# A one-core decoder layer: context values as 32-column weights, no transposes of the attention result, and four work lists rewritten

## What is computed

```python
x = x + gated_linear_attention(layernorm(x), ...)   # conv, silu, 8 heads, causal, decay
x = x + xattn(layernorm(x), ctx, ctx, Wq, Wk, Wv, Wo)
x = x + ffn(layernorm(x), w_router, w_block)        # the best 48 of 64 positions only

# xattn, 16 heads of 8 features:
q = heads(Q @ Wq.T); k = heads(K @ Wk.T); v = heads(V @ Wv.T)
attn = softmax(q k^T / sqrt(8))
return merge(attn @ v) @ Wo.T
```

## Time and profile before

| | |
|---|---|
| median of 3 runs | 335.04 us |
| profiled execution | 332.23 us |
| its span, first to last instruction | 330.5 us |
| PE busy / DVE / ACT / POOL | 274.6 / 240.0 / 245.9 / 163.7 us |
| mean granted PE clock | 0.985 |

### The profile page before, as it was taken

One profiled execution on the slowest core, in us unless ns is written; L12 is line 12 of the kernel. 1 busy time (PEld: TensorE's weight loads), 2 busy tenths in 40 slices (PEclk: granted clock), 3 DMA queues, 4 the chain that ended last, 5 costly groups with the idle time before them and its releaser, 6 DMA issues.

```text
span 330.5 us, 10717 instructions
## 1 busy us (share of the span) xinstructions
PE 274.6 (83%) x4184; PEld 195.9 (59%) x4184; DVE 240.0 (73%) x588; ACT 245.9 (74%) x438; POOL 163.7 (50%) x226
## 2 busy tenths in 40 slices
PE   1697868879998899888999899889987997898861
PEld 1576636655677566655776478556854684465540
DVE  1577788689578968896789677976697657656554
ACT  6399868976988698769976997699769875862611
POOL 5145366834755445574657375728551625023630
PEclk9998999999999999999999999999999999999996
DMA  3830200020003000300020001300110010001010
GB/s 73 234 99 18 67 0 6 13 69 2 4 13 86 2 3 12 96 10 1 11 73 4 0 10 33 93 1 9 33 45 2 5 43 16 2 0 34 2 32 17
DMA packets 15730, 10.52 MB, mean 32 GB/s; under 512 B 2816, under 2 KB 13952, under 8 KB 15680
## 3 DMA queue, kind: packets, MB, share of 16 engines
q1 hardware_dynamic: 15680, 9.84, 11.2%
HBM read 4.79 MB, written 2.10 MB: 21 GB/s over the span
## 4 chain that ended last, share of the span: by engine, by line
PE 34%; issue 13%; DVE 13%; ACT 12%; POOL 7%; POOLq 0%; ACTq 0%; DVEq 0%
PE S L824 6%; PE PT L861 6%; PE PB L882 6%; ACT pr L1259 3%; PE PA L766 3%; ACT prT L1266 3%; ACT L1183 2%; PE S L839 2%; DVE nmax L1627 2%; DVE at L1573 2%; PE PT L646 2%; PE PA L782 2%; POOL rs L399 2%; POOL yout L523 2%; DVE st L1476 1%
## 5 line engine op out<-in xcount | busy, mean ns | idle before, releaser
L1627 DVE TENSOR_REDUCE nmax<-S 128x16 bf16<-128x1024 f32 x31 | 37.9, 1221 | 29.0 <-PE S L824 29.0
L1266 ACT COPY prT<-PT 128x512 f32<-128x512 f32 x62 | 36.1, 582 | 15.8 <-PE PT L861 14.8
L861 PEld LDWEIGHTS PT<-ident,pr 128*128 128x128 f32 x248 | 26.4, 140 | 29.0 <-issue 17.8
L861 PE MATMUL PT<-ident,pr 128*128 128x128 f32 x248 | 39.9, 283 | 4.2 <-ACT prT L1266 2.3
L1147 ACT ACTIVATE k_bd<-S,k_rows 128x512 f32<-128x512 f32 (+1 forms) x72 | 41.9, 645 | 0.4 <-PE S L671 0.2
L824 PE MATMUL S<-k_bd,qT 64*64 64x512 f32 x248 | 33.7, 613 | 5.5 <-ACT pr L1259 2.6
L882 PE MATMUL PB<-v_x,prT 128*64 128x18 f32 x992 | 37.3, 213 | 0.5 <-ACT prT L1266 0.2
L882 PEld LDWEIGHTS PB<-v_x,prT 128*64 128x64 f32 x992 | 32.8, 137 | 8.1 <-issue 6.8
L1259 ACT ACTIVATE pr<-S,rs 128x1024 f32<-128x1024 f32 x31 | 34.5, 1114 | 3.4 <-PE S L839 2.7
L486 POOL TENSOR_TENSOR kc<-ke,e_r 128x512 f32<-128x512 f32 x32 | 34.9, 1109 | 3.7 <-issue 3.7
L766 PEld LDWEIGHTS PA<-v_bd,at 128*64 128x64 f32 x512 | 16.6, 137 | 19.4 <-DVE at L1573 13.9
(11 more groups left out here) (171 smaller groups left out, 669.1 us busy)
## 6 DMA issues: line engine op xcount, KB each, us to landing
cT<-in_ctxT SPq DMA_DIRECT2D x7, 256.0 KB, 3.6
v_bd<-vt SPq DMA_DIRECT2D x28, 64.0 KB, 2.1
out<-yout SPq DMA_DIRECT2D x7, 256.0 KB, 3.8
q_bd<-qs SPq DMA_DIRECT2D x96, 8.0 KB
cT<-in_ctxT SPq DMA_DIRECT2D x2, 128.0 KB, 2.6
x_all<-in_x SPq DMA_DIRECT2D x1, 256.0 KB, 2.9
v_bd<-vt SPq DMA_DIRECT2D x8, 32.0 KB, 2.1
out<-yout SPq DMA_DIRECT2D x2, 128.0 KB, 3.3
```

The costliest lines, as they stand in the source:

```text
L861: last = nc.tensor.transpose(dst[:, P * p:P * p + P], pr_v[:, i % 2, P * (hp * n + p):P * (hp * n + p) + P], ident[:, :])
L1266: nc.scalar.copy(prT[:, 512 * n:512 * n + 512], pt_buf(g, n)[:, :]).then_inc(s_prT, 1)
L1627: nc.vector.tensor_reduce(nmax[:, XH * (i % 2):XH * (i % 2) + XH], cut(s_buf(g, i), XH, L), AX.X, ALU.max, negate=True).then_inc(s_max, 1)
```

## The change

The operands of `x_values` change places: `v_x` is the weight, 32 columns per head pair, and a piece of `prT`, 64 columns, is the stream. Four head pairs of a half fill the four 32-row bands of `PB`, so the result has features as rows. The 16 values of a pair stand in columns 16 to 31 of its 32, with zeros ahead of them; half n = 0 reads a window 16 columns further on, so that the two halves fall on different rows of a band and are accumulated. A second weight, `den_of` (ones and zeros), with all 128 columns of `prT` as the stream, writes each feature's denominator beside it. Per half there are 12 matmuls where there were 8.

```diff
-                for p in range(hp * n, hp * n + hp):
-                    for half in range(2):
-                        last = nc.tensor.matmul(dst[L * half:L * half + L, 2 * VC * p:2 * VC * p + 2 * VC],
-                                                prT_v[:, p, L * half:L * half + L], v_xv[:, g % 2, 2 * i + half, p, :],
-                                                start=True, stop=True)
+                ahead = VB // 2 * (1 - n)
+                for half in range(2):
+                    for q in range(hp):
+                        p = hp * n + q
+                        nc.tensor.matmul(dst[VB * q:VB * q + VB, L * half:L * half + L],
+                                         v_xs[:, g % 2, 2 * i + half, VB * p + ahead:VB * p + ahead + VB],
+                                         prT_v[:, p, L * half:L * half + L],
+                                         start=n == 0 and half == 0, stop=n == 1, skip_group_check=True)
+                for q in range(hp):
+                    last = nc.tensor.matmul(dst[VB * q:VB * q + VB, P:2 * P], den_of[:, ahead:ahead + VB],
+                                            prT_v[:, hp * n + q, :], start=False, stop=n == 1, skip_group_check=True)
                 last.then_inc(s_PV, 1)
 
-            def x_out(g):
-                pe.wait_ge(s_cx, start(g + 1))
-                pe.wait_ge(s_prT, 2 * start(g + 1))
-                to_features(g, PT, cx).then_inc(s_CX, 1)
-
             def x_out2(g):
-                pe.wait_ge(s_cxT, g + 1)
+                pe.wait_ge(s_cx, start(g + 1))
...
-            def b_out(g):
-                act.wait_ge(s_CX, g + 1)
-                nc.scalar.copy(cxT[:, 0:cols(g)], PT[:, 0:cols(g)]).then_inc(s_cxT, 1)
...
-                nc.vector.reciprocal(mine, pv[:, :, XD:VC]).then_inc(s_rden, 1)
+                mine = rden[:, P * (i % 2):P * (i % 2) + P]
+                nc.vector.reciprocal(mine, pv[:, P:2 * P]).then_inc(s_rden, 1)
                 dve.wait_ge(s_rden, start(g) + i + 1)
                 if i == 0:
-                    dve.wait_ge(s_CX, g)
-                nc.vector.tensor_tensor(cx[:, E * i:E * i + E].rearrange("p (h v) -> p h v", h=XH), pv[:, :, 0:XD],
+                    dve.wait_ge(s_WO, g)
+                nc.vector.tensor_tensor(cxT[:, P * i:P * i + P], pv[:, 0:P], mine, ALU.mult).then_inc(s_cx, 1)
```

More of the change, by code:

```diff
@@ L984, in first @@
                 attend(1, 1, 1)
+                project_g(2)
+                x_scores(0, 1)
+                x_attend(0, 0, 0)
+                less_max(0, 1)
+                x_attend(0, 0, 1)
+                project_v(2)
+                x_values(0, 0, 0)
+                context_values(2)
+                aug_weights(2)
+                x_values(0, 0, 1)
                 x_attend(0, 1, 0)
-                project_v(2)
-                x_values(0, 0, 1)
+                context_keys(2)
                 x_attend(0, 1, 1)
+                transpose_o(1)
                 x_values(0, 1, 0)
                 x_values(0, 1, 1)
-                context_values(2)
-                aug_weights(2)
-                context_keys(2)
-                x_out(0)
-                project_g(2)
-                transpose_o(1)
-                x_out2(0)
                 gla_out(1)
                 transpose_x(3)
+                x_out2(0)
                 queries(1)
@@ L1034, in step @@
                 x_scores(n, 3)
+                x_values(n, 1, 1)
                 x_attend(n, 2, 0)
-                x_values(n, 1, 1)
-                x_attend(n, 2, 1)
-                less_max(n, 3)
                 if has(a + 1):
                     transpose_x(a + 1)
+                less_max(n, 3)
+                x_attend(n, 2, 1)
+                gla_out(b)
                 x_values(n, 2, 0)
@@ L1094, in last @@
                 keep_awake(8, 20)
-                x_out(7)
+                queries(8)
                 x_out2(7)
-                queries(8)
-                keep_awake(8, 21)
                 queries2(8)
@@ L1124, in last @@
                 ffn(8)
+            def last():
+                pass
             run(first, opening, step, closing, last)
@@ L1310, in opening @@
                 a_keys(0, 0)
+                a_values(0)
+                a_keys(0, 1)
                 a_qk(0)
@@ L1367, in opening @@
                 a_v(2)
-                a_square(1)
                 b_probs(0, 1, 1)
-                a_spread(1)
-                a_deviation(1)
-                a_values(2)
-                b_out(0)
                 a_keys(2, 0)
-                a_gates(2)
+                a_keys(2, 1)
                 a_features(3)
+            def opening():
+                pass
             def step(n):
                 a, b, c = n + 2, n + 1, n - 1
-                a_keys(b, 1)
                 a_gate(b)
@@ L1383, in step @@
                 a_keys(b, 2)
+                a_keys(b, 3)
                 b_queries2(n)
+                a_values(b)
                 a_aug(b)
-                a_keys(b, 3)
                 a_silu(a)
@@ L1461, in last @@
                 b_probs(8, 1, 1)
-                b_out(8)
                 b_ffn(8)
@@ L1914, in closing @@
                 b_own(7)
-            def last():
                 b_ranks(7)
```

484 lines of the change are left out of this document (236 added, 248 removed).

## The result

The changed kernel takes 342.4 us (median of 4 runs, 341.1 to 344.6) where the kernel before took 334.3 beside it: a ratio of 1.027, 95% interval 1.022 to 1.032. It is slower. The forecast was 331 us where the profiled execution before had 332.2, so no change that can be told; 342.4 lies near the upper end of the whole range, which the slower rivals held, but outside the forecast's own, 326 to 338, and the time moved the other way.

What follows compares the result with a forecast made beforehand. No engine is full; a chain through several engines around the never-free score buffer sets the step. Opening -1.5, loop +0.1 and end +0.3 gave -1.1 us on 332.2: 331 us, range 322 to 343.

Steps and rivals of the forecast that it cites:

- the opening part: Everything ahead of step 1: DVE's wait for x_rest given back, then 3.9 us instead of 5.44 after scores(2, 0); -1.5 us.
- five terms: Changes to the score buffer's five uses per step: +0.3, -0.4, +0.4, +0.8 and -1.0 us, summing to 0.1 over six steps.
- tile 1: Second use of the score buffer: maximum waits behind head norm, yet 6.3 us against 6.74, -0.4; sign, DVE wait near 2 us.
- tile 0: First use of the score buffer: PE's work between successive scores takes 5.6 us against 5.34, +0.3.
- tile 2: Third use of the score buffer: next scores wait for x_values(n, 1, 0), which needs tile 0 weighed; 5.05 us against 4.64, +0.4.
- The end: From weighing the last tile to the last x_out2: longer weighing and a selection stand ahead on DVE, +0.3 us.
- The reciprocal: On DVE, growing from 16 to 128 elements per row: 0.95 us each, 2.8 us more DVE work per step.
- The swapped matmuls: A half of x_values on PE with four bands side by side: 0.5 us, +0.04; 0.65 to 0.7 in a single run.
- The cheap reciprocal: Rival: the longer reciprocal on DVE costs only 0.37 us, giving 324 us; chance 0.16.
- Two bands at a time: Rival: only two PE bands run side by side, 0.9 us a half, +0.45, giving 342 us; chance 0.10.
- DVE as the bound: Rival: half of DVE's new 2.8 us a step does not fit its waits, +1.4 a step, 339 us; chance 0.16.
- Better lists: Rival: the new order hides more, without the tiles' waits, -1.1 us a step, 324 to 325 us; chance 0.12.

Runs made afterwards that it cites:

- e14: The changed kernel itself, unedited, measured again beside the other runs: 342.3 us, ratio 1.025 to the kernel before.
- e6: Changed kernel with a_stats(2) on DVE and scale_a(2) on POOL moved later, as in the kernel before, so nothing ahead waits for x_rest: 340.2 us, 1.020.
- e9: Changed kernel with POOL's kc products of group 1 waiting for group 2's silu, and scores(1, 0) later on PE: 340.7 us, 1.023.
- e4: Changed kernel with a reciprocal of 128 x 16 elements in place of 128 x 128, the other divisors being ones: 333.4 us, 0.998.
- e12: Changed kernel with POOL's first kc of a step also waiting for DVE's gl of that step: 342.9 us, 1.031.
- e8: Kernel before, with old operands and short reciprocals, in the new instruction lists: 341.8 us, 1.024.
- e1: Kernel before with the swapped matmuls, long reciprocal and wider clear in its old lists, x_out and b_out taken out: 333.6 us, 1.001.
- e11: Kernel before with a reciprocal of 128 x 128 elements in place of 128 x 16, the added results read by nobody: 343.6 us, 1.033.
- e10: Changed kernel with the edits of e6 and e9 together: 338.2 us, 1.017.
- e2: Changed kernel with the opening part's lists of the kernel before and the new lists from step 1 on: 350.1 us, 1.048.

## Why the prediction was wrong, step by step

**The step that failed** is the opening part: "gives the 2.5 us back, so these transfers start at the same time by my walk", priced at -1.5 us, measured +5.75 (4.6 between the means under e14). The transfers start 7.37 us late. The walk had seen DVE's wait for `x_rest` rightly (4.42 us at 14.8 to 19.2), but it is not given back: without it the transfers start 2.6 us earlier and step 1 1.4 to 2.5 us earlier (e6). The walk had left out the head norm and the maximum that now stand between `a_log(2)` and `a_scaled_q(2)`, 2.0 us by the rows of both kernels. And it had carried over each duration from the trace of before without asking what POOL does at that moment in the new order; e9 shows 2.9 us of that at the silu, but not at the transfers, where e9 holds up the masks instead. How much of it reaches step 1 is open, and so is what the stretch at 1.2 GHz adds. The last piece was well walked: of 3.9 us from `scores(2, 0)` to `x_scores(1, 0)`, 4.99 were measured in the first profile and 4.05 in e14.

**The loop.** Each of the five terms has the right sign, and is within 0.3 us: +0.13 for +0.3, -0.44 for -0.4, +0.67 for +0.4, +0.59 for +0.8, -0.82 for -1.0 in step 3. The sign that was given for tile 1, a DVE wait at the second maximum, is not there: DVE waits 1.03 us ahead of the head norm, for `attend`, and the maximum comes as late as walked. The sum of six steps is 3 us nonetheless, not 0.1, for step 3 of the first profile, with its +0.13, does not stand for six: in e14 the six are 0.55, 0.38, 0.37, 0.47, 0.57 and 0.68 us longer than before. Step 4 there has 34.64 us, before 34.17: tile 0 is +0.49 for +0.3 and tile 2 +0.68 for +0.4, with the rest as walked. Tile 2 is the term that the long reciprocal lengthens; e4 has 4.60 there, before 4.63.

**Step 7** was not priced (+1.10), though it has the same reciprocals: e4, without the long ones, has 26.27 us there instead of 28.49. **The end** was +0.59 in the first profile and -0.11 in e14, for +0.3.

**The reciprocal** is right to the percent: 951 ns for 0.95. Against the 254 of the earlier trace rows it is 6.2 ns per element, where 5.9 had been estimated. The estimate of 1.2 us, worked out from the Trainium skill's repeat count ("VectorE: DVE Perf Modes", on a lane's resources), was too long; the measurement decides.

**The swapped matmuls** are right as well. A half in a single run takes 0.65 us, from 63.99 to 64.64, where 0.5 was taken and 0.65 to 0.7 named as the sign:

```profile
63.99 0.43 PE L882 MATMUL PB<-prT,v_x 128*32 128x64 f32 x16
64.24 0.40 PE L887 MATMUL PB<-prT,den_of 128*32 128x128 f32 x8
```

**The rivals.** The cheap reciprocal fell by its size, but its price was good: 7 us forecast, 9 in e4. Two bands at a time fell (0.65 us a half, not 0.9); that its 342 meets the measured time is luck. DVE as the bound came near, with 339, by another road too: 31.45 of 34.40 us are busy, yet e12 takes 0.78 us a step from DVE and steps 3 to 6 are no shorter than in e14. Better lists fell: e8. No rival had the opening part in it, and that is where the measured time lies.

## What to carry to other kernels

A change that swaps one cost for another must be priced at both ends on the path: here the transposes' 10 us and the reciprocal's 10 us cancel, and only e1 with e11 showed it. When an order is redrawn, durations don't move with the instructions: look up, for each vector instruction that the path goes through, what POOL runs beside it in the new place, and what now stands ahead of it in its own list. And walk the part ahead of the loop as closely as the loop, from the first late landing on: what is late there was not made up for by any step behind it.

## What the runs showed of the hardware

In these traces a DVE instruction on SBUF data takes longer beside POOL's `kc`. `gl` takes 0.68 us alone and 1.46 when a `kc` began 0.16 us ahead; the first convolution, with one tensor as input, has a mean of 912 ns where it had 524. The Trainium skill says this in "SBUF — State Buffer", "Who interferes with whom": an instruction of DVE with two inputs in SBUF contends with one of POOL that reads SBUF, one in a mode with two ports with any of POOL's, and the one that comes second is blocked while the first has the shared ports. No run here shows in which mode the first convolution ran. If `gl` had waited to the end of `kc`, that would have been 0.92 us more; the trace shows 0.78, so it agrees nearly. It does not agree for POOL's small power instruction, as far as POOL's spans can be trusted: it ran first here in the kernel before, with `xcT` at its usual 0.68 us beside it:

```profile
213.26 1.01 POOL L443 TENSOR_TENSOR rs<-ve,minus_half 128x4 f32<-128x4 f32 x1
...
213.50 0.68 DVE L1516 SCALAR_TENSOR_TENSOR xcT<-th,y 128x512 f32<-128x512 f32 x1
```

The other surprise is the clock in the opening part: after PE's wait of 2.35 us for the silu the stretch 50 to 56 us was granted 0.50, the 1.2 GHz level, and `x_scores(0, 0)` took 1.99 us. In e10 PE waits 1.42 us there, the granted clock is 0.63 from 45 to 47.2 and 0.55 from 47.2 to 49.2 us, with `x_scores(0, 0)` at 1.93 us, and 1.00 behind that. The wait alone doesn't tell whether it comes: e1 and e2 make the same calls up to step 1, and in both PE waits 1.35 us for a maximum at about 45 us; behind it e1 was granted 0.67 in the stretch 45 to 50 us and e2 1.00, and step 1 starts at 76.19 and 74.27.
